# Decoder layer on one core: queries turned unscaled, their scales applied in the exponentials, output parts split later

## What is computed

```python
x = x + _L0_attn_ref(_layernorm(x, axis=-1), ...)                 # ends with out @ o_proj_w.T
x = x + _L0_xattn_ref(_layernorm(x, axis=-1), ctx_2048, ...)
# inside the cross attention, 16 query heads, 4 key heads, head size 128:
q = (draft_hidden @ Wq.T).reshape(bsz, draft_len, H, HD)
q = _rms_norm(q, q_norm_w).transpose(0, 2, 1, 3)   # w * (q * rsqrt(mean(q*q) + EPS)), per row and head
q = _rope(q, draft_position_ids)
scores = jnp.einsum('bhqd,bhkd->bhqk', q, k) * SCALE
probs = jax.nn.softmax(scores, axis=-1)
```

## Time and profile before

| | us |
|---|---|
| median of 3 runs | 2493.8 (2493.62 to 2494.19) |
| profiled execution | 2492.17 |
| its span (first to last instruction) | 2490.5 |
| first output stage in it, first matmul to the next stage's first instruction | 585.4 to 1026.8 |
| cross attention | 1026.8 to 1960 |

### The profile page before, as it was taken

One profiled execution on the slowest core, in us unless ns is written; L12 is line 12 of the kernel. 1 busy time (PEld: TensorE's weight loads), 2 busy tenths in 40 slices (PEclk: granted clock), 3 DMA queues, 4 the chain that ended last, 5 costly groups with the idle time before them and its releaser, 6 DMA issues. The chain is left out here.

```text
span 2490.5 us, 35704 instructions
## 1 busy us (share of the span) xinstructions
PE 2181.5 (88%) x10448; PEld 1664.9 (67%) x10448; DVE 1309.4 (53%) x2830; ACT 1020.9 (41%) x2184; POOL 887.9 (36%) x906
## 2 busy tenths in 40 slices
PE   5689999995789989599999999999999799749991
PEld 3578888874577777366666666666666588637771
DVE  3635555555766666444454545454555256535554
ACT  2313333333344444345555555555555322125660
POOL 2400000002555555534232323323235255446664
PEclk8889999997899999799999999999999999869996
DMA  7621211134344444332222222222221344154336
GB/s 284 170 71 38 67 36 61 38 109 142 105 123 123 126 128 151 113 110 73 66 58 65 74 58 77 58 65 58 65 58 38 92 114 118 51 198 135 101 106 194
DMA packets 289858, 243.77 MB, mean 98 GB/s; under 512 B 147842, under 2 KB 254834, under 8 KB 286322
## 3 DMA queue, kind: packets, MB, share of 16 engines
q1 hardware_dynamic: 269122, 190.19, 26.0%
q10 hardware_dynamic: 14160, 34.22, 3.8%
q0 software_dynamic: 6496, 18.37, 2.8%
HBM read 149.31 MB, written 93.42 MB: 97 GB/s over the span
## 5 line engine op out<-in xcount | busy, mean ns | idle before, releaser
L2234 DVE TENSOR_REDUCE ca_down<-ca_ps_s 112x1 f32<-112x487 f32 x256 | 164.6, 661 | 308.5 <-PE ca_ps_s L2047 306.4
L1971 POOL TENSOR_TENSOR ca_k<-ca_k 125x512 f32<-125x512 f32 x64 | 81.2, 1269 | 541.4 <-DVE ca_k L2219 541.4
L2047 PE MATMUL ca_ps_s<-ca_kT,ca_qT 128*112 128x487 f32 x512 | 230.5, 572 | 0.8 <-issue 0.8
L2136 ACT ACTIVATE ca_prob<-ca_ps_s,ca_down 112x487 f32<-112x487 f32 x256 | 169.8, 666 | 135.2 <-DVE ca_down L2234 131.1
L75 PE MATMUL out_ps_y<-out_w_hi,out_o_hi 128*128 128x512 f32 x448 | 189.2, 422 | 33.7 <-DVE out_w_lo L1288 18.9
L2063 PE MATMUL ca_ps_o<-ca_pT,ca_v 125*128 125x448 f32 (+1 forms) x512 | 203.2, 539 | 0.6 <-ACT ca_pT L2143 0.6
L75 PE MATMUL ca_ps_p<-ca_w_hi,ca_c_hi 128*125 128x512 f32 x384 | 174.0, 453 | 23.1 <-POOL ca_c_lo L1965 23.1
L76 PE MATMUL out_ps_y<-out_w_lo,out_o_hi 128*128 128x512 f32 x448 | 182.1, 406 | 0.0
L77 PE MATMUL out_ps_y<-out_w_hi,out_o_lo 128*128 128x512 f32 x448 | 181.6, 405 | 0.0
L599 POOL COPY sa_val<-lat_v 112x128 f32<-112x128 f32 (+1 forms) x64 | 18.9, 296 | 411.2 <-PE sa_ps_o L656 410.9
L2063 PEld LDWEIGHTS ca_ps_o<-ca_pT,ca_v 125*128 125x128 f32 (+1 forms) x512 | 97.1, 190 | 100.9 <-issue 100.1
(11 more groups left out here) (291 smaller groups left out, 5671.5 us busy)
## 6 DMA issues: line engine op xcount, KB each, us to landing
self_outT<-sa_ov SPq DMA_DIRECT2D x64, 224.0 KB, 2.4
out_o_raw<-self_outT SPq DMA_DIRECT2D x56, 256.0 KB, 3.0
cross_qT<-out_qt SPq DMA_DIRECT2D x56, 256.0 KB, 2.5
ca_qT<-cross_qT SPq DMA_DIRECT2D x64, 224.0 KB, 2.8
cross_outT<-ca_ov SPq DMA_DIRECT2D x64, 224.0 KB, 3.0
out_o_raw<-cross_outT SPq DMA_DIRECT2D x56, 256.0 KB
ffn_raw<-in_expert_w SPq DMA_DIRECT2D x8, 1536.0 KB, 7.0
ca_c_first<-in_ctxT SPq DMA_DIRECT2D x15, 750.0 KB
```

What stands on the lines that cost most here:

```text
L1971: pool.tensor_tensor(k1[0:m, :], k1[0:m, :], k2[0:m, :], ALU.add).then_inc(k_added.sem, 1)
L2047: pe.matmul(ps_s[j % 2][:, :], qT[i % 2][:, j, :], kT[par][:, i, :], start=True, stop=True).then_inc(scored.sem, 1)
L2136: act.activation(prob[j][:, 0:KV], ps_s[j % 2][:, :], ACT.Exp, bias=down[:, j:j + 1], accum_out=total[:, j:j + 1]).then_inc(exped.sem, 1)
L2234: dve.tensor_reduce(down[:, j:j + 1], ps_s[j % 2][:, :], AX.X, ALU.max, negate=True).then_inc(maxed.sem, 1)
```

## The change

It has three parts, and what they need.

1. The queries are transposed and stored unscaled. POOL's factors go in a tile [128, 16] per row tile, one store per tile to a new tensor `q_scales` (SP, `store_s`). Cross attention loads them per batch (`load_s`); VectorE multiplies minus the maximum of the raw scores by the row's factor (`top` to `down`, one more instruction per head), and the exponential takes the factor as its `scale`.
2. The hi and lo parts of groups 2 and 3 of an output tile are made one body later; in `body` the orders of ACT and VectorE are written anew. On VectorE the angles stand between rotate 0 and rotate 1 (before: after rotate 1), and a low part stands behind them.
3. On VectorE `guest.prepare` stands behind the split of the weights (before: first). SP's `guest.load` waits for the memset in it.

```diff
@@ self_output: sync
+            def store_s(t, par):
+                wait(sp, q_rooted, t, NQ - 1)
+                carry(sp, t, ticks)
+                sp.dma_start(q_scales[bass.ds(t * P, P), :], rstd[par][:, :]).then_inc(s_put[par].sem, 16)
                 if not first:
                     store_q(t - 1, 3)
+                    store_s(t - 1, 1 - par)
                 if ahead:
                     load(t + 2, 3)
@@ self_output: gpsimd
-            def unit(t, i):
-                a, b, par = q1[i][:, :], q2[i % 2][:, :], i % 2
+            def unit(t, i, h, par):
+                a, b, head = q1[i][:, :], q2[i % 2][:, :], slice(i * HQ, (i + 1) * HQ)
                 wait(pool, q_rot, t, i)
                 pool.tensor_tensor(a, a, b, ALU.add).then_inc(q_added.sem, 1)
                 wait(pool, q_sum, t, 2 * i + 1)
-                wait(pool, q_ready, t, i - 2)
-                pool.tensor_tensor(rstd[par][:, :], ssum[par][:, :], minus_half[:, :], ALU.pow).then_inc(q_rooted.sem, 1)
+                if i == 0:
+                    wait(pool, s_put[par], h, -1)
+                    carry(pool, t, pool_ticks)
+                pool.tensor_tensor(rstd[par][:, head], ssum[i % 2][:, :], minus_half[:, :], ALU.pow).then_inc(q_rooted.sem, 1)
@@ self_output: scalar
-            def scale(t, i):
-                wait(act, q_added, t, i)
-                wait(act, q_rooted, t, i)
-                for j in range(HQ):
-                    head = q1[i][:, j * HD:(j + 1) * HD]
-                    ins = act.activation(head, head, ACT.Copy, scale=rstd[i % 2][:, j:j + 1])
-                ins.then_inc(q_ready.sem, 1)
-
                 else:
                     square(t - 1, 3)
-                if ahead:
-                    high(t + 2, 0)
-                if not first:
-                    scale(t - 1, 2)
+                    if not last:
+                        high(t + 1, 2)
                 square(t, 0)
-                if ahead:
-                    high(t + 2, 1)
-                if not first:
-                    scale(t - 1, 3)
+                if not first and not last:
+                    high(t + 1, 3)
                 square(t, 1)
                 if not first:
                     keep(t - 1, 2)
-                scale(t, 0)
                 if ahead:
-                    high(t + 2, 2)
+                    high(t + 2, 0)
+                    high(t + 2, 1)
                 if not first:
                     keep(t - 1, 3)
                 guest.sine(act, t + 2, par)
-                scale(t, 1)
                 keep(t, 0)
-                if ahead:
-                    high(t + 2, 3)
                 square(t, 2)
                 keep(t, 1)
@@ self_output: vector
                 else:
                     rotate(t - 1, 3, 1 - par)
+                if not first and not last:
+                    low(t + 1, 2)
+                rotate(t, 0, par)
+                guest.angles(dve, t + 2, par)
+                if not first and not last:
+                    low(t + 1, 3)
+                rotate(t, 1, par)
                 if ahead:
                     low(t + 2, 0)
-                rotate(t, 0, par)
-                if ahead:
                     low(t + 2, 1)
-                rotate(t, 1, par)
-                if ahead:
-                    low(t + 2, 2)
-                guest.angles(dve, t + 2, par)
                 if not last:
                     add(t + 1, h + par, 1 - par)
                     scale(t + 1, 1 - par)
-                if ahead:
-                    low(t + 2, 3)
                 rotate(t, 2, par)
 
-            guest.prepare(dve)
             for h in range(H):
...
+            guest.prepare(dve)
             add(0, 0, 0)
@@ self_output: tensor
             def turn_q(t, i):
-                wait(pe, q_ready, t, i)
+                wait(pe, q_added, t, i)
@@ cross_attention: sync
+            def load_s(b, par):
+                sp.dma_start(scales[par][:, :], q_scales[bass.ds(b * S, S), :]).then_inc(s_in[par].sem, 16)
                 if not first:
                     store(b - 1, 3)
+                if more:
+                    load_s(b + 1, 1 - par)
@@ cross_attention: scalar
                 act.activation(prob[j][:, 0:KV], ps_s[j % 2][:, :], ACT.Exp, bias=down[:, j:j + 1],
+                               scale=scales[par][:, n:n + 1],
                                accum_out=total[:, j:j + 1]).then_inc(exped.sem, 1)
@@ cross_attention: vector
-                dve.tensor_reduce(down[:, j:j + 1], ps_s[j % 2][:, :], AX.X, ALU.max, negate=True).then_inc(maxed.sem, 1)
+                dve.tensor_reduce(top[:, j:j + 1], ps_s[j % 2][:, :], AX.X, ALU.max, negate=True).then_inc(topped.sem, 1)
+                if n == 0:
+                    wait(dve, s_in[par], h)
+                wait(dve, topped, b, n)
+                dve.tensor_tensor(down[:, j:j + 1], top[:, j:j + 1], scales[par][:, n:n + 1], ALU.mult).then_inc(maxed.sem, 1)
```

More of the change, by code:

```diff
@@ L927, in load, with self_output @@
         eng.dma_start(self.w_raw[:, 1, :, :], wvT).then_inc(self.w_in[1], 16)
-def self_output(nc, oT, ahead_of, res, store_x, store_xT, qT, rope, following):
+def self_output(nc, oT, ahead_of, res, store_x, store_xT, qT, q_scales, rope, following):
     ctx = Phase(nc, "out1")
@@ L958, in self_output @@
         ssum = [sb(f"ssum{i}", [P, HQ]) for i in range(2)]
-        rstd = [sb(f"q_rstd{i}", [P, HQ]) for i in range(2)]
+        rstd = [sb(f"q_rstd{i}", [P, H]) for i in range(2)]
         qt = [sb(f"qt{i}", [P, HQ, P]) for i in range(2)]
@@ L988, in self_output @@
         q_put = [ev(f"qT_stored{i}", NQ // 2, 1, 16) for i in range(2)]
-        ticks = ctx.sem("ticks")
+        s_put = [ev(f"q_scales_stored{i}", 1, 1, 16) for i in range(2)]
+        ticks, pool_ticks = ctx.sem("ticks"), ctx.sem("pool_ticks")
         guest = RopeTables(ctx, *rope)
@@ L998, in _ @@
                 q_put[i].open(sp)
+                s_put[i].open(sp)
             def load(t, c):
@@ L1147, in keep, with body @@
                 act.activation(qt[i % 2][:, :, :], ps_r[i % 2][:, :, :], ACT.Copy).then_inc(q_kept.sem, 1)
-            def body(t, h, par, ahead=True, first=False):
+            def body(t, h, par, ahead=True, first=False, last=False):
                 turn(t, h, par)
@@ L1198, in _ @@
             following.load(act)
-            body(TT - 1, TT // 2 - 1, 1, ahead=False)
+            body(TT - 1, TT // 2 - 1, 1, ahead=False, last=True)
             square(TT - 1, 3)
             for i in (2, 3):
-                scale(TT - 1, i)
                 keep(TT - 1, i)
@@ L1777, in cross_output, with cross_attention @@
     return ctx
-def cross_attention(nc, ahead_of, ctxT, xT_hi, xT_lo, tables, qT_src, oT, next_w):
+def cross_attention(nc, ahead_of, ctxT, xT_hi, xT_lo, tables, qT_src, q_scales, oT, next_w):
     M = (CT, CT, CT, S)
@@ L1803, in cross_attention @@
         prob = [sb(f"prob{j}", [S, 4 * CT]) for j in range(HQ)]
+        top = sb("top", [S, HQ])
         down = sb("down", [S, HQ])
+        scales = [sb(f"scales{i}", [S, H]) for i in range(2)]
+        s_in = [ev(f"scales_loaded{i}", 1, step=16) for i in range(2)]
         total = sb("total", [S, HQ])
@@ L1937, in _ @@
             load(0, 0, 0)
+            load_s(0, 0)
             load_q(0, 0)
@@ L2169, in step @@
                     next_w.load(act, i)
-                exp(b, i, 0)
-                exp(b, i, 1)
+                exp(b, i, 0, par)
+                exp(b, i, 1, par)
                 if more:
@@ L2179, in step @@
                 copy_pT(b, i, 1)
-                exp(b, i, 2)
-                exp(b, i, 3)
+                exp(b, i, 2, par)
+                exp(b, i, 3, par)
                 if more:
@@ L2254, in step @@
                     rotate(b + 1, h + par, i, 1 - par)
-                maximum(b, i, 0)
-                maximum(b, i, 1)
+                maximum(b, h, i, 0, par)
+                maximum(b, h, i, 1, par)
                 if more:
@@ L2260, in step @@
                 divide(b, i, 1)
-                maximum(b, i, 2)
-                maximum(b, i, 3)
+                maximum(b, h, i, 2, par)
+                maximum(b, h, i, 3, par)
                 divide(b, i, 2)
@@ L2687, in build @@
     clear(nc, fold, lat, sa)
-    out1 = self_output(nc, o1T, out_w, x_rows, x1, x1T, qT,
+    out1 = self_output(nc, o1T, out_w, x_rows, x1, x1T, qT, q_scales,
                        (pos_ctx, pos_x, pos_rows, inv_freq, k_norm, q_norm, tables), cross_w)
     cross_out_w = CrossOutputWeights(nc, xwoT)
-    ca = cross_attention(nc, cross_w, ctxT, *x1T, tables, qT, o2T, cross_out_w)
+    ca = cross_attention(nc, cross_w, ctxT, *x1T, tables, qT, q_scales, o2T, cross_out_w)
     clear(nc, out_w, out1, cross_w, ca)
```

22 lines of the change are left out of this document (12 added, 10 removed).

## The result

The kernel after takes 2461.89 us (median of 4, 2452.19 to 2466.22), the kernel before beside it 2493.71 (4, 2493.27 to 2494.19): **0.9867 of before, 95% interval 0.9837 to 0.9897**, 31.8 us less. Faster, as forecast (the prediction set 5 us as what can be told apart), and 1.5 us from the predicted 2460.4. Four executions of the kernel after spread over 14 us, so a hit this close is in part luck. The profiled execution took 2460.55 us, its span is 2458.8.

What follows compares the result with a forecast made beforehand. PE was taken to bound the kernel, full in cross attention but waiting in the first output stage. Terms 30.9 - 0.7 + 1.3 + 2.2 + 0.6 - 0.9 = 33.4 us gave 2460.4 us; range 2444 to 2478.

Steps and rivals of the forecast that it cites:

- What bounds the stage: First output stage: PE waits 16.4 us before turned queries, 9.8 before normalised rows in ten tiles; lateness begins at ACT's load waits.
- PE's own work, 24.76 us a tile: First output stage: PE needs 24.76 us a tile, read from tile 12; 3.9 us a tile are waits and slow clock.
- The new wait, 1.1 us a tile: Before the fourth projection PE waits 1.1 us for low 3, delayed by POOL's tables meeting the angles; bounds 0 and 2.3.
- long-lock rival: First output stage: POOL's power holds VectorE too, wait 2.2 us, twelve tiles 13.2 us worse, 2474 us; chance 0.13.
- Tile 12, +0.7: Tile 12 of the first output stage, without high parts to make, goes from 25.20 to 25.86 us: 0.7 lost.
- Tile 0, 1.3: First output stage, tile 0: only the scale leaves the way to its first transposes; 1.3 us gained, bounds 0 and 3.
- last tile, 2.2: End of the first output stage: the last rotation starts 2.2 us earlier with angles before rotate 1; bounds 0 and 5.
- Start, 0.6: Start of the first output stage: prepare behind the weights' low parts gains 0.6 us; bounds 4 gained, 3 lost.
- Cross attention, +0.9: Cross attention: the added multiplications cost nothing in 60 of 64 steps, 0.9 us in the last batch; bounds 0.2 to 2.5.
- over 0.6 us as a sign of being wrong: Cross attention: a multiplication of 112x1 taking over 0.6 us would show the prediction wrong; the nearest row took 0.16.
- one multiplication is added to each: Cross attention's last batch: each of four 1.44 us PE waits before the transposes grows by one multiplication; 0.9 us lost.
- Nothing behind cross attention: Second output stage and experts, behind cross attention: predicted difference 0.

Runs made afterwards that it cites:

- order_only: Only the new orders of ACT and VectorE put into the kernel before, scales kept on ACT, cross attention as before: 2453.5 us, 0.986 of before.
- scales_only: The change with only the queries' scales moved, the orders and the place of prepare as before: 2478.7 us, 0.997 of before.
- tables_sooner: The change with POOL's tables ahead of the addition of group 0 instead of behind it: 2448.1 us, 0.985 of before.
- order_tables_splits: order_only with POOL's tables ahead of group 0's addition and the next weights' splits out of cross attention's last batch: 2446.3 us, 0.983 of before.
- both repeats: The changed kernel run twice more without edits, each with its own trace: 2452.2 and 2455.3 us, 0.986 and 0.989 of before.
- splits_earlier: The change with POOL's splits of the next weights moved from cross attention's last batch to batches 1 and 14: 2450.7 us, 0.986 of before.
- after: The changed kernel as first measured and traced against the kernel before: 2461.89 us, 0.9867 of before.
- after_beside: The changed kernel run again without edits, the second repeat: 2455.3 us, 0.989 of before.

## Why the prediction held, point by point

**What bounds the stage.** Right in the main. Both of PE's waits of the earlier trace rows went. The orders alone take away both (order_only), the scales alone only the one before the turned queries (scales_only). That ACT's wait for loads was the root, rather than the late angles, isn't shown: order_only removes both.

**PE's own work, 24.76 us a tile.** 24.60 to 24.67 by the two kernels without waits, tables_sooner and order_tables_splits: 0.1 too much, 1 to 2 us over eleven tiles. In part by luck: it was read from tile 12, which had lost 0.4 us that no wait shows and has 0.2 to 0.3 less work than the others (24.40 in both kernels).

**The new wait, 1.1 us a tile.** Mechanism right, shown by tables_sooner; size off: 0.69 (25.36 - 24.67). The lay-out put the end of low 3 at T+16.4, it came at T+16.0: rotate 0 started 0.2 earlier (803.06, T+7.06), and the angles ended 7.3 us after it, not 8.25. The row that was used, the tables' start to the last angle's end, 4.43 us, has pieces of another pairing; in the steady tile it is 3.3. With the term above this is the 5.5 us that tiles 1 to 11 gained beyond the sum. The long-lock rival falls again: POOL's power of 4 columns runs beside angles of the usual 0.33 (from 806.02 to 807.09 beside those at 806.24 and 806.60 in the change, from 808.80 to 810.12 beside the one at 809.75 in tables_sooner). The Trainium skill (SBUF — State Buffer, "SBUF: two separate sides") has the shared pair locked for the whole instruction. The rows agree for POOL's products and additions here, and not for this power.

**Tile 12, +0.7.** It lost nothing (25.2 as before). Its new wait is 0.5 us, and with the tables sooner it takes 24.4, so the meeting costs it 0.8; but it had lost as much before, 0.44 that a wait shows and 0.4 that none does. A term of 0.7 too many.

**Tile 0, 1.3; last tile, 2.2.** 2.2 (2.65 in both repeats) and 4.8 (6.3 in both repeats). Tile 0 and the first trace's last tile are inside their bounds of 3 and 5, the repeats' last tile isn't. At the end rotate 1 started 7.2 us after rotate 0, not 8.4, and the clock, 0.83 in the second 10 us behind the last turn before, was 1.00 there; the order alone gives 1.9 us there, the scales alone 2.5.

**Start, 0.6.** About 1, in scatter of 1; the hand-over from one wait to the next is as described.

**Cross attention, +0.9.** The failed step: 7.2 us, outside its bounds of 0.2 to 2.5. Ahead of the last batch the cost is next to nothing, as said, even though about once a step, at head 0, the multiplication meets POOL's addition and takes some 0.75 us. The prediction had named over 0.6 us as a sign of being wrong, and that POOL idles there as an argument; both came out against it, at no cost, since heads 0 and 1 have the wider cover. This one ends 0.01 after the addition:

```profile
1859.41 0.76 DVE L2243 TENSOR_TENSOR ca_down<-ca_top,ca_scales 112x1 f32<-112x1 f32 x1
```
```profile
1858.89 1.27 POOL L1975 TENSOR_TENSOR ca_k<-ca_k 112x512 f32<-112x512 f32 x1 [6.91 <-DVE ca_k L2224]
```

In the last batch "one multiplication is added to each" was too simple. Three things were left out: that POOL splits the next weights there, so that multiplications take up to 0.74 and divisions 1.05 where PE has no projections to hide them (half of the loss, splits_earlier; the kernel before had divisions of 0.56 and 1.14 there already, which could have been read); that the exponential's operand costs 0.09 us; and that the longer waits came with a lower clock of PE, in one step and at the very end. The Trainium skill has the second (ScalarE: Activation LUTs, "What ACT_TABLE_LOAD costs"): each operand with a value per partition adds about 93 ns to an ACTIVATE. The rows agree, 667 to 757 ns. Worked out from that figure, an estimate, the last batch loses 0.1 a step to it, which is what the steps show (0.28 = 0.19 + 0.09).

**Nothing behind cross attention.** In the first trace 6.3 us were lost there; the repeats put most of it to chance. A part stays open. The four traces without the scales' tensor but with the new order took 242.6 to 243.2 us in the second output stage, the nine with it 245.2 to 254.4 (seven of them 246.8 to 249.1). PE's waits for the places of the experts' rows were 11.1 to 14.9 us in the nine, 10.3 in three of the four and 11.3 in the fourth; the kernel before took 246.0 us, with 11.6 of them. Whether the new tensor does this, or how the stage starts against its transfers, no run tells.

**The total.** 33.4 predicted, 31.7 in the profiled pair: the first output stage gave 43.5 us where 34.3 were forecast, 1.8 came ahead of it, and 13.6 were lost behind it where 0.9 were forecast. So the sum came out by cancellation, which is luck; its parts in the first output stage were right in kind, and it was off by 5.5 us in tiles 1 to 11 and 6 in cross attention.

## What to carry to other kernels

Work moved under an engine that is full costs nothing only where it is full: look for the batch, tile or tail in which the cover is missing, list everything that other engines do there, and price the added operation beside their longest instruction. Before moving arithmetic to take it off a late engine, ask whether that engine is late for its work or for its order: here a new order without the move gave the same time, and the move's gain was spent in the next stage. And a job of POOL's that has time (the tables, the splits) should stand where VectorE reads PSUM or rests, or where PE has work to hide the meeting; not where VectorE works from SBUF on what PE waits for next.

## What the runs showed of the hardware

- An exponential of 112x487 with a scale per partition takes 0.757 us, with bias alone 0.667.
- A VectorE multiplication of 112x1 (0.16 us) that meets a POOL addition of 128x512 waits for its end: 0.76 us, ending 0.01 us after it. A power of 4 columns on POOL, 1.3 us long, doesn't hold VectorE's operations beside it (0.33 to 0.48), and POOL's tables don't hold a rotation that reads PSUM (two products of 128x256 from 803.75, 0.75 us together, beside a table product from 803.72 to 805.02 in tables_sooner, and 0.75 as well at 798.60, where POOL rests).
- In the last batch one PE wait of 2.9 us instead of 1.4 came with a granted clock of 0.83 over 10 us and a step 3.3 us longer; with waits of 1.7 the clock stayed at 1.00 there, but was 0.71 in the last 8 us. The last weighting took 4.97 us with waits of 1.53 to 1.72 us ahead of it and 3.28 with waits of 1.44.
- Times of one program differ by up to 19 us between executions on one chip (2442.9 to 2462.2), while tiles 1 to 11 and cross attention repeat within 0.3 us; what varies is the start and the end of the first output stage (1 to 2 us), the second output stage (246.8 to 254.4 in three traces of the change) and the experts (270.7 to 280.3 in all traces), where PE waits 39 to 47 us for the loads of rows (after, after_beside, splits_earlier), and the stages ahead of the first output stage (573.7 to 580.8).
